# Attention stage of a four-layer graph network: rows of two tiles in every twelve picked on TensorE instead of two in sixteen, and the picked keys' product 128 columns wide

## The chip, the core and the metric

The kernel runs on one core of one Trainium2 chip. The metric is the device time of one execution in microseconds (us); lower is better.

## What is computed

Four layers of a graph network run on 3,125 nodes with 64 features and on 103,125 edges (two directions of 50,000 and one loop per node), sorted by their target node. Before each layer the nodes are normalised and cut at zero, and each layer's result is added to the nodes. The third layer is the attention that the change touches. Cut to what matters:

```python
q = (h @ Wq + bq).reshape(n, HEADS, C)
k = (h @ Wk + bk).reshape(n, HEADS, C)
v = (h @ Wv + bv).reshape(n, HEADS, C)
e = (edge_attr @ We).reshape(-1, HEADS, C)
qi, kj, vj = q[tgt], k[src] + e, v[src] + e
alpha = jnp.sum(qi * kj, axis=-1) / math.sqrt(C)
ex = jnp.exp(alpha - segment_max(alpha, tgt, n)[tgt])
a = ex / (segment_sum(ex, tgt, n)[tgt] + 1e-08)
agg = segment_sum(a[:, :, None] * vj, tgt, n)
```

For every edge the row of its source node (`src`) is needed; these are the rows that are gathered or picked.

## The kernel before, in words

The stages run one after the other: tables, dense matrices of the graph, layers 0 and 1, the attention's tables, the attention over the edges (`stage_attend`), the node part (`stage_nodes`), the messages of the last layer (`stage_messages`), and the output. The change lies in `stage_attend` and in the constants in front of it.

`stage_attend` cuts the edges into T1 = 403 tiles of 256 edges. A block is 64 target nodes, of which there are J2 = 49. A table made earlier lists V2 = 451 visits, each one tile with one block. Every engine walks the visits in a loop over `i`, with its own offsets: in iteration `i`, TensorE turns tile `t = i + 2`, scores visit `i`, makes picking products that belong to that iteration, and sums visit `i - 5`. I call one such iteration a step.

A tile gets the rows of its source nodes in one of two ways.

- Fetched tiles: GpSimd issues two indirect DMAs of 128 rows each from the row table in memory (L1594). A ring of eight semaphores lets it run at most eight fetched tiles ahead of what TensorE has turned (L1591), and another wait keeps it within the 64 tile slots (L1592). TensorE waits for the landing and for the edge attributes (L1617, L1618), and turns the tile with two transposes (L1620); ScalarE copies the result into `XF` (L1672).
- Picked tiles: the last two of every AG = 16 tiles, from tile 16 on (`picked`, L1321 to L1323), which makes 24 groups with 48 such tiles; the other 355 tiles are fetched. For a group the 512 source indices are loaded to all partitions as 256 KB by a DMA of SP (L1579), ScalarE turns them to float16 (L1687), VectorE compares them with the node numbers of each of the 25 chunks of 128 nodes (L1765, one 128x512 comparison each, eight buffers), and TensorE multiplies each result with that chunk of a table that holds every value as two float16 halves (L1645, 128x512, 25 of them into one bank). ScalarE copies the sum out (`hT`, L1694). In the step of the tile TensorE adds the two halves by a product with `comb`, two identities of 64x64 on top of each other: once with the 64 features on the partitions, for the keys (L1612), and twice with the edges on the partitions (L1614). ScalarE scales both into `XF` (L1669) and `rows` (L1670). The attributes of a picked tile come to `XF` by a DMA of SP (L1574).

`picks_of_step` (L1335 to L1338) spreads the 25 comparisons and products of a group over AG - 2 steps, starting PICK_AHEAD = 4 steps ahead of the group's first tile; the loads, the conversion L1687 and the copy L1694 have their steps by the same constants.

The rest of a step is the same for every tile. TensorE transposes the weights of the visit three steps behind (L1625), adds the mask of the block (two products, L1634), the scores (L1637), and sums with two products (L1655; before a picked tile's sum it waits for that tile's copy, L1652). VectorE makes the mask (L1712), the maximum (L1739), three small updates (L1745, L1750, L1759) and the sum (L1756). ScalarE copies the weights (L1675) and takes the exponentials (L1680, L1681). SP loads the queries (L1584) and the edge attributes (L1571).

Float32 products issue two matmuls each in the trace, so L1637 appears twice in a step and L1655 four times.

The constants of the schedule are these; nothing is planned by costs:

```python
AG = 16
AHOT = 8
TURN_AHEAD = 2
PICK_AHEAD = 4
```

`stage_messages` has a picking scheme of its own (GP = 6), which the change leaves alone; only its semaphore offsets Q0 and N0 follow the number of groups in `PICKS`.

Of the kernel before, what the change touches and what calls it, by code (L numbers as in the profile page):

```python
# [8 lines left out]
F16 = mybir.dt.float16  # L9
# [8 lines left out]
P = 128  # L18
NODES = 3125
EDGES = 103125  # L20
D = 64
# [7 lines left out]
TE = 256  # L29
# [43 lines left out]
RT = 64  # L73
# [1183 lines left out]
ONE = D + DE  # L1257
# [5 lines left out]
def landed(t, each=1):  # L1263

    return (t // R + 1) * (16 * each)
# [27 lines left out]
def wait(eng, sem, n):  # L1293

    if not isinstance(n, int) or n > 0:
        eng.wait_ge(sem, n)
# [10 lines left out]

CENTER = NODES // 2
SHIFTS = 5
AG = 16  # L1310
AHOT = 8
TURN_AHEAD = 2
MASK_AHEAD = 4
# [1 line left out]
SUM_BEHIND = 5  # L1315
# [5 lines left out]
def picked(t):  # L1321

    return t >= AG and t % AG >= AG - 2 and t - t % AG + AG <= T1  # L1323


FETCHED = [t for t in range(T1) if not picked(t)]
PICKS = [t for t in range(0, T1, AG) if picked(t + AG - 2)]


def fetched_before(t):  # L1330

    return sum(not picked(u) for u in range(t))


def picks_of_step(i):  # L1335

    return [(q, a) for q, t in enumerate(PICKS) for u in range(AG - 2) if i == t - PICK_AHEAD + u
            for a in range(u * NCH // (AG - 2), (u + 1) * NCH // (AG - 2))]  # L1338


def step_of_tile(t):

    return t + 1


def step_of_weights(v):

    return v + P_BEHIND + TURN_AHEAD + 1
# [162 lines left out]
def stage_attend(nc, m, keep, x_out, q_out, ea, ea_t, src, x_t, q_t):  # L1511
# [4 lines left out]
    with ExitStack() as ctx:  # L1516
        sem = lambda n: ctx.enter_context(nc.semaphore(n))
        take = Take(m.big)
# [6 lines left out]
        XF = take(RT * TE).rearrange("p (t e) -> p t e", t=RT)  # L1525
# [7 lines left out]
        psK = [m.PB[i][0:XW, 0:TE] for i in range(2)]  # L1533
# [3 lines left out]
        psR = [m.PB[5 + i][:, TE:TE + 2 * D].rearrange("p (s d) -> p s d", s=2) for i in range(2)]  # L1537
        psH = m.PB[7]
        hT = take(TE).bitcast(F16)
        key = take(TE).bitcast(F16)  # L1540
        comb = take(D // 2).bitcast(F16)
        down, wexp = take(1), take(1).bitcast(I32)
        keyI = more(2 * TE).bitcast(I32)
        hot = [more(TE).bitcast(F16) for _ in range(AHOT)]
# [18 lines left out]
        @block.sync  # L1563
        def _(sp):
            own = Walk(nc, m, "block", mybir.EngineType.SP)
            for v in range(V2):
                if v < T1:
                    wait(sp, turned, step_of_tile(v - R))
                    wait(sp, summed, v - RT + J2)
                    tile = ea[v:v + 1, :, :].rearrange("t p n -> p (t n)").rearrange("p (s c) -> p s c", s=2)  # L1570
                    sp.dma_start(rows[:, v % RT, :, D:D + DE], tile).then_inc(m.landed_e[v % R], 16)  # L1571
                    if picked(v):
                        sp.wait_ge(init, 2)
                        sp.dma_start(XF[D:D + DE, v % RT, :], ea_t[v, :, :]).then_inc(landed_x[v % 2], 16)  # L1574
                    if v + PICK_AHEAD in PICKS:
                        q = PICKS.index(v + PICK_AHEAD)
                        wait(sp, key_ready, q)
                        edges = src[(v + PICK_AHEAD + AG - 2) * TE:(v + PICK_AHEAD + AG) * TE]
                        sp.dma_start(keyI, edges.partition_broadcast(P)).then_inc(key_landed, 16)  # L1579
                j = own.of(v)  # L1580
                wait(sp, scored, v - R + 1)
                if v == 0:
                    sp.wait_ge(q_out, 16 * NG)
                sp.dma_start(qT[v % R], q_t[bass.ds(j, 1), :, :].rearrange("j p n -> p (j n)")).then_inc(m.landed_q[v % R], 16)  # L1584
# [12 lines left out]
        @block.tensor  # L1597
        def _(pe):
            pe.wait_ge(init, 1)
            own = Walk(nc, m, "slot", mybir.EngineType.PE)  # L1600
            for i in range(-TURN_AHEAD, V2 + SUM_BEHIND):
                t, u = i + TURN_AHEAD, i - P_BEHIND
                if u < V2:
                    wait(pe, copied, t - 1)
                if t < T1 and picked(t):
                    q = PICKS.index(t - t % AG)
                    e = (t % AG - (AG - 2)) * TE
                    pe.wait_ge(m.landed_e[t % R], landed(t))
                    pe.wait_ge(landed_x[t % 2], LATE_LOADS[t % 2] + 16 * (q + 1))
                    pe.wait_ge(h_copied, q + 1)  # L1610
                    wait(pe, acc_ready, i - SUM_BEHIND - 1)
                    pe.matmul(psK[t % 2][0:D, :], comb, hT[:, e:e + TE], start=True, stop=True)  # L1612
                    for s in range(2):
                        ins = pe.matmul(psR[(i - SUM_BEHIND) % 2][:, s, :], hT[:, e + s * P:e + (s + 1) * P], comb, start=True, stop=True)  # L1614
                elif t < T1:
                    n = fetched_before(t)
                    pe.wait_ge(m.landed_g[n % R], landed(n, 2))  # L1617
                    pe.wait_ge(m.landed_e[t % R], landed(t))  # L1618
                    for s in range(2):
                        ins = pe.transpose(psK[t % 2][:, s * P:(s + 1) * P], rows[:, t % RT, s, :], m.ident[:, :])  # L1620
                if 0 <= u < V2:
                    pe.wait_ge(exp_ready, u + 1)
                    for s in range(2):
                        part = slice(s * P, (s + 1) * P)
                        ins = pe.transpose(psT[t % 2][:, part], Pm[u % 6][:, part], m.ident[:, :])  # L1625
                if u < V2:
                    ins.then_inc(turned, 1)
                v = i
                if 0 <= v < V2:
                    slot = own.of(v)  # L1630
                    pe.wait_ge(oh_ready, v + 1)
                    wait(pe, exp_ready, v - 2)
                    for e in range(2):
                        pe.matmul(psS[v % 3][:, e * P:(e + 1) * P], oh[v % 8][:, e, :], pen, start=(e == 0), stop=False)  # L1634
                    pe.wait_ge(m.landed_q[v % R], landed(v))
                    pe.wait_ge(copied, step_of_tile(min(v, T1 - 1)))
                    pe.matmul(psS[v % 3], qT[v % R][0:XW, :], XF[0:XW, bass.ds(slot, 1), :].rearrange("p t e -> p (t e)"),  # L1637
                              start=False, stop=True).then_inc(scored, 1)
                for q, a in picks_of_step(i):
                    n = q * NCH + a  # L1640
                    if a == 0:
                        pe.wait_ge(init, 2)
                        wait(pe, h_copied, q)
                    pe.wait_ge(hot_ready, n + 1)
                    pe.matmul(psH, table[:, a, :, :].rearrange("p s d -> p (s d)"), hot[n % AHOT],  # L1645
                              start=(a == 0), stop=(a == NCH - 1)).then_inc(hot_used, 1)
                v = i - SUM_BEHIND
                if 0 <= v < V2:
                    slot = own.of(v)
                    pe.wait_ge(copied, step_of_weights(v))  # L1650
                    if t < T1 and picked(t):
                        pe.wait_ge(copied, step_of_tile(t))  # L1652
                    wait(pe, acc_ready, v - 1)
                    for s in range(2):
                        ins = pe.matmul(psA[v % 2], PT[v % 4][:, s * P:(s + 1) * P],  # L1655
                                        rows[:, bass.ds(slot, 1), s, :].rearrange("p t c -> p (t c)"), start=(s == 0), stop=(s == 1))
                    ins.then_inc(summed, 1)
# [39 lines left out]
        def _(dve):  # L1697
# [18 lines left out]
            def split():  # L1716

                dve.wait_ge(q_out, 16 * NG)
                for t in range(AG - 2, RT, AG):
                    dve.memset(XF[ONE:ONE + 1, t:t + 2, :], 1.0)  # L1720
                dve.tensor_copy(down, downI)
                dve.tensor_copy(comb[0:D, :], m.ident[0:D, 0:D])
                dve.tensor_copy(comb[D:P, :], m.ident[D:P, D:P])
                chain(dve.tensor_scalar(wexp, gall.bitcast(I32), 0x7F800000, None, ALU.bitwise_and))
                chain(dve.tensor_scalar(wexp, wexp, float(87 << 23), None, ALU.max))
                chain(dve.tensor_scalar(m.scale.bitcast(I32), wexp, -1.0, float(268 << 23), ALU.mult, ALU.add))
                chain(dve.tensor_scalar(m.unscale.bitcast(I32), wexp, -float(14 << 23), None, ALU.add))
                chain(dve.tensor_scalar(table[:, :, 0, :], hn, m.scale, None, ALU.mult))
                dve.scalar_tensor_tensor(table[:, :, 1, :], hn, m.scale, table[:, :, 0, :], ALU.mult, ALU.subtract).then_inc(init, 1)

            for i in range(-MASK_AHEAD, V2 + SUM_BEHIND):
                if i == 3:
                    split()
# [650 lines left out]
```

## Time and profile before

| | |
|---|---|
| device time, three runs | 3196.3, 3214.78 and 3215.32 us, median 3214.78 us |
| profiled execution, first to last instruction | 3198.0 us |
| mean granted clock of TensorE in it | 0.937 |
| attention: first to last gather issued | 1390.3 to 2280.5 us |
| attention: fetched / picked tiles | 355 / 48 |

The page gives the profiled execution's span alone as its time. PE is TensorE's matmuls, PEld its weight loads, DVE is VectorE, ACT ScalarE, POOL GpSimd, SP SyncE. A busy share counts instructions, not issuing of DMAs; the indirect DMAs of GpSimd are shown as instructions of that engine.

### The profile page before, as it was taken

What the parts mean: (1) busy time and instruction counts of PE and PEld (TensorE: products, weight loads), DVE (VectorE), ACT (ScalarE), POOL (GpSimd) and SP (SyncE); (2) the same over time, 40 slices, a digit from 0 to 9 for tenths busy, and PEclk for the clock granted to TensorE, in tenths of its full rate; (3) what the DMA queues carried; (4) which work ended last, traced back from release to release, by engine and by line L of the source; (5) the groups of instructions that cost most, each with busy time, mean ns of one, the idle gap of its engine ahead of it and who ended that gap; (6) DMA issues with size and microseconds to landing.
All of it is one profiled execution on the core that took longest, in us unless ns stands there. A gap on an engine that the chain in (4) does not pass through costs nothing. (4 is left out here: it accounts for less than half of the span.)

```text
span 3198.0 us, 70441 instructions
## 1 busy us (share of the span) xinstructions
PE 2723.7 (85%) x18621; PEld 1834.2 (57%) x18621; DVE 2250.6 (70%) x6702; ACT 1612.0 (50%) x4685; POOL 1512.6 (47%) x1604
## 2 busy tenths in 40 slices
PE   2777777799998499759888888998986999999998
PEld 1566665355554244337777777776874555555556
DVE  6999998566665312657777777777887777777772
ACT  1788887033332000035555555555664666666666
POOL 2121122044443000067777777777405777777770
PEclk6999999899999799869999999999997999999995
DMA  1122222056557755543333333333203555445540
GB/s 38 73 91 89 91 89 89 21 195 204 196 197 257 270 238 238 223 102 80 84 81 81 82 85 79 83 83 82 63 21 98 127 131 131 127 128 130 131 112 12
DMA packets 446966, 378.15 MB, mean 118 GB/s; under 512 B 174376, under 2 KB 385416, under 8 KB 446632
## 3 DMA queue, kind: packets, MB, share of 16 engines
q1 hardware_dynamic: 396184, 315.64, 32.3%
q0 software_dynamic: 40896, 43.60, 6.7%
q10 hardware_dynamic: 9552, 14.75, 1.3%
q8 instruction: 175, 2.87, 0.4%
q14 instruction: 159, 1.30, 0.1%
HBM read 286.75 MB, written 87.03 MB: 117 GB/s over the span
## 5 line engine op out<-in xcount | busy, mean ns | idle before, releaser
L1594 POOL DMA_INDIRECT big<-row_table,src x710 | 675.0, 951 | 217.1 <-issue 171.6
L2080 POOL DMA_INDIRECT big<-message_table,src x542 | 532.6, 983 | 228.2 <-issue 154.2
L2119 PE MATMUL banks<-big 128*128 128x512 f16 x1650 | 422.6, 380 | 8.9 <-DVE big L2194 8.9
L2212 DVE TENSOR_SCALAR big<-big 128x2048 f16<-128x2048 f16 (+2 forms) x396 | 422.4, 1067 | 1.3 <-DMA big<-shifted_keys 0.7
L507 PE MATMUL banks<-work 128*128 128x226 f16 x1197 | 312.3, 261 | 104.2 <-ACT banks L538 41.4
L899 PE MATMUL banks<-big,work 128*128 128x512 f16 (+1 forms) x1750 | 350.0, 359 | 17.0 <-DVE work L1041 17.0
L964 POOL TENSOR_TENSOR work<-work 128x400 f16<-128x400 f32 x196 | 180.2, 945 | 280.5 <-DVE work L1033 220.3
L1739 DVE TENSOR_REDUCE big<-banks 128x1 f32<-128x256 f32 x451 | 190.2, 422 | 173.1 <-PE banks L1637 159.7
L1637 PE MATMUL banks<-big 97*128 x902 | 303.4, 419 | 0.7
L508 PE MATMUL banks<-work 128*128 128x200 f16 x1197 | 300.5, 251 | 0.0
L509 PE MATMUL banks<-work 128*128 128x200 f16 x1197 | 298.6, 249 | 0.0
L450 POOL COPY work<-work 128x100 f16<-128x100 f16 x120 | 86.2, 723 | 380.9 <-DVE work L473 361.8
L1680 ACT ACTIVATE big<-big 128x1 f32<-128x1 f32 x451 | 91.6, 203 | 346.5 <-DVE big L1750 336.2
L899 PEld LDWEIGHTS banks<-big,work 128*128 128x128 f16 x1750 | 157.9, 101 | 188.2 <-DVE work L1041 17.3
L2156 ACT ACTIVATE big<-iotaH,rel 128x64 f32<-128x64 f16 x902 | 258.5, 334 | 5.5 <-DVE big L2171 3.9
L2128 PEld LDWEIGHTS banks<-big 128*64 128x64 f32 x1804 | 148.4, 145 | 184.9 <-issue 183.9
L1115 PE MATMUL banks<-big,work 128*128 128x512 f16 x900 | 202.7, 386 | 55.8 <-DVE work L1199 52.0
L1620 PE MATMUL banks<-ident,big 128*97 128x128 f32 x710 | 145.9, 288 | 100.0 <-issue 68.2
L928 ACT CAST work<-work 128x400 f16<-128x400 f32 x196 | 100.8, 525 | 238.8 <-DMA work<-weights_dense 238.0
L2128 PE MATMUL banks<-big 128*64 x1804 | 212.5, 244 | 7.8 <-issue 2.8
L2119 PEld LDWEIGHTS banks<-big 128*128 128x128 f16 x1650 | 153.4, 98 | 114.2 <-DVE big L2194 9.2
L533 ACT ACTIVATE work<-banks 128x800 f32<-128x800 f32 x196 | 163.5, 834 | 97.7 <-PE banks L509 89.9
(373 smaller groups left out, 6143.4 us busy)
## 6 DMA issues: line engine op xcount, KB each, us to landing
big<-weights_halves SPq DMA_DIRECT2D x10, 6400.0 KB, 24.0
big<-shifted_keys SPq DMA_DIRECT2D x66, 640.0 KB
weights_dense<-work SPq DMA_DIRECT2D x196, 200.0 KB, 1.9
work<-weights_dense SPq DMA_DIRECT2D x196, 200.0 KB, 2.7
weights_halves<-work SPq DMA_DIRECT2D x98, 400.0 KB, 2.9
big<-q_table SPq DMA_DIRECT2D x451, 64.0 KB
big<-in_ef SPq DMA_DIRECT2D x403, 64.0 KB
big<-in_ea SPq DMA_DIRECT2D x403, 32.0 KB
```

Of the source, the lines that this page charges most:

```text
L507: pe.matmul(to(CW, CW + CAW), rows[:, 0, t, :], cols[:, t, :], start=False, stop=True, skip_group_check=True)
L508: pe.matmul(to(0, CW), rows[:, 1, t, :], cols[:, t, 0:CW], start=False, stop=True, skip_group_check=True)
L509: pe.matmul(to(0, CW), rows[:, 2, t, :], cols[:, t, 0:CW], start=False, stop=True, skip_group_check=True).then_inc(vis_done, 1)
L899: ins = pe.matmul(m.PB[c % 4][:, 0:width(c)], z[k][:, a, :, :], m.counts(c)[:, a, :], start=(a == 0), stop=(a == NCH - 1))
L1115: pe.matmul(out, z[l % 2][:, a, :, :], weights[:, :, s, a * BP:(a + 1) * BP], start=(a == 0 and s == 0), stop=False)
L1594: po.indirect_dma_start(rows[:, t % RT, s, 0:D], None, x_t.rearrange("a p c -> (a p) c"), bass.IndirectOffsetOnAxis(ap=m.src2[:, s, t:t + ...
L1637: pe.matmul(psS[v % 3], qT[v % R][0:XW, :], XF[0:XW, bass.ds(slot, 1), :].rearrange("p t e -> p (t e)"), start=False, stop=True).then_inc( ...
L2080: po.indirect_dma_start(G[n % R][:, s, :], None, g_t.rearrange("a p c -> (a p) c"), bass.IndirectOffsetOnAxis(ap=m.src2[:, s, t:t + 1], ax ...
L2119: pe.matmul(psH[q % 2], table[:, a, :, :].rearrange("p s d -> p (s d)"), hot[:, 2 * TE * a:2 * TE * (a + 1)], start=(a == 0), stop=(a == N ...
L2128: ins = pe.matmul(psA[v % 3], oh[v % 4][:, s, :], M[:, bass.ds(slot, 1), s, :].rearrange("p t c -> p (t c)"), start=(s == 0), stop=(s == 1))
L2156: ins = nc.scalar.activation(away[v % 2][:, s, :], m.iotaH[:, 0:BD], ACT.Abs, bias=m.rel2[:, s, v:v + 1], scale=-1.0)
L2212: dve.tensor_scalar(hot[:, 2 * TE * a:2 * TE * (a + n)], key[q % 2][:, 0:n, :], place[:, BATCHES.index((a, n)):BATCHES.index((a, n)) + 1], ...
```

## The change

One constant goes from 16 to 12. The two picked tiles are then the last two of every twelve tiles, from tile 12 on: 32 groups with 64 picked tiles, and 339 fetched ones. A group's 25 comparisons and 25 products are spread over ten steps (two and three in turn) instead of fourteen. `comb` is twice as wide (the two identities also side by side), so that the keys' product writes all 128 partitions of its bank, of which ScalarE reads the first 64 as before; the product for the rows uses the first 64 columns. The memsets that put the constant row into `XF` follow the new places; four are left in number.

```diff
-AG = 16
+AG = 12
...
-        comb = take(D // 2).bitcast(F16)
+        comb = take(D).bitcast(F16)
...
-                    pe.matmul(psK[t % 2][0:D, :], comb, hT[:, e:e + TE], start=True, stop=True)
+                    pe.matmul(m.PB[t % 2][:, 0:TE], comb, hT[:, e:e + TE], start=True, stop=True)
                     for s in range(2):
-                        ins = pe.matmul(psR[(i - SUM_BEHIND) % 2][:, s, :], hT[:, e + s * P:e + (s + 1) * P], comb, start=True, stop=True)
+                        ins = pe.matmul(psR[(i - SUM_BEHIND) % 2][:, s, :], hT[:, e + s * P:e + (s + 1) * P], comb[:, 0:D], start=True, stop=True)
...
-                for t in range(AG - 2, RT, AG):
-                    dve.memset(XF[ONE:ONE + 1, t:t + 2, :], 1.0)
+                for t in range(RT):
+                    if picked(t) and t % 2 == 0:
+                        dve.memset(XF[ONE:ONE + 1, t:t + 2, :], 1.0)
                 dve.tensor_copy(down, downI)
-                dve.tensor_copy(comb[0:D, :], m.ident[0:D, 0:D])
-                dve.tensor_copy(comb[D:P, :], m.ident[D:P, D:P])
+                for half in range(2):
+                    dve.tensor_copy(comb[0:D, half * D:(half + 1) * D], m.ident[0:D, 0:D])
+                    dve.tensor_copy(comb[D:P, half * D:(half + 1) * D], m.ident[D:P, D:P])
```

## Rows read from the trace of the kernel before

**Rows 1.** The page's first line: span and instructions.

```profile
span 3198.0 us, 70441 instructions
```

**Rows 2.** Windows: busy us (instructions) of PE, PEld, DVE, ACT, POOL; PE clock, DMA share, GB/s.

```profile
1500.00:2200.00 700.00, 623.31 (x4368) 503.32 (x4367) 532.46 (x2733) 396.16 (x1356) 529.77 (x559) 0.98 0.39 82
2290.00:2350.00 60.00, 59.70 (x474) 55.42 (x473) 57.87 (x326) 38.88 (x143) 0.00 (x0) 1.00 0.17 47
```

**Rows 3.** The gathers' line L1594: durations, first and last start; idle (us, times).

```profile
L1594 POOL DMA_INDIRECT big<-row_table,src x710: 940/944/1870, 1390.3 to 2280.5; - x178
...
  issue: 171.6, 563
  PE banks L1655: 29.0, 95
```

**Rows 4.** Timeline of GpSimd: start, duration, instruction; in brackets the idle time ahead.

```profile
1395.52 0.94 POOL L1594 DMA_INDIRECT big<-row_table,src  x1 [0.30 <-issue]
1396.77 0.94 POOL L1594 DMA_INDIRECT big<-row_table,src  x1 [0.31 <-issue]
...
1949.27 0.94 POOL L1594 DMA_INDIRECT big<-row_table,src  x1 [0.30 <-issue]
1950.52 0.94 POOL L1594 DMA_INDIRECT big<-row_table,src  x1 [0.31 <-issue]
...
1954.26 0.94 POOL L1594 DMA_INDIRECT big<-row_table,src  x1 [0.30 <-issue]
```

**Rows 5.** Timeline of TensorE: steps of fetched tiles, with two products L1645 and with one.

```profile
1933.20 0.38 PE L1620 MATMUL banks<-ident,big 128*97 128x128 f32 x2
...
1934.24 0.60 PE L1645 MATMUL banks<-work 128*128 128x512 f16 x2
...
1935.09 0.38 PE L1620 MATMUL banks<-ident,big 128*97 128x128 f32 x2
...
1936.13 0.38 PE L1645 MATMUL banks<-work 128*128 128x512 f16 x1
...
1936.76 0.38 PE L1620 MATMUL banks<-ident,big 128*97 128x128 f32 x2
```

**Rows 6.** Timeline of TensorE: last two fetched tiles of a group and its picked ones.

```profile
1887.69 0.39 PE L1620 MATMUL banks<-ident,big 128*97 128x128 f32 x2
...
1891.37 0.27 PE L1612 MATMUL banks<-big 128*64 128x256 f16 x1 [0.58 <-ACT big L1694]
...
1893.27 0.68 PE L1655 MATMUL banks<-big,work 128*128 x4 [0.41 <-ACT big L1675]
...
1895.82 0.68 PE L1655 MATMUL banks<-big 128*128 x4 [0.19 <-ACT work L1675]
1896.34 0.39 PE L1620 MATMUL banks<-ident,big 128*97 128x128 f32 x2
```

**Rows 7.** Timeline of TensorE: the turns of tiles 250 and 252.

```profile
1951.91 0.43 PE L1620 MATMUL banks<-ident,big 128*97 128x128 f32 x2 [0.48 <-issue]
...
1958.53 0.43 PE L1620 MATMUL banks<-ident,big 128*97 128x128 f32 x2 [2.15 <-issue]
```

**Rows 8.** Lines L1612, L1645, L1765 and L1687: ns min/median/max, first and last start.

```profile
L1612 PEld LDWEIGHTS banks<-big x48: 106/106/128, 1469.6 to 2280.8; 128*64 128x64 f16 x48
L1612 PE MATMUL banks<-big x48: 269/297/423, 1469.6 to 2280.8; 128*64 128x256 f16 x48
...
L1645 PE MATMUL banks<-work x600: 377/381/634, 1431.3 to 2274.1; 128*128 128x512 f16 x150
...
L1765 DVE TENSOR_SCALAR work<-big x600: 273/284/523, 1427.8 to 2271.8; 128x512 f16<-128x512 f16 x150
...
L1687 ACT ACTIVATE big<-work,big x24: 707/710/711, 1426.3 to 2239.6; 128x512 f16<-128x512 int32 x24
```

**Rows 9.** Timeline of VectorE: from one maximum to the next, with two comparisons between.

```profile
1938.24 0.41 DVE L1739 TENSOR_REDUCE big<-banks 128x1 f32<-128x256 f32 x1
...
1939.89 0.42 DVE L1739 TENSOR_REDUCE big<-banks 128x1 f32<-128x256 f32 x1
```

## The prediction, written before the changed kernel ran

> **What bounds the kernel now.** I read the span first, then the busy shares by stretch, then the line of the gathers with its idle time, and last the timelines of GpSimd and TensorE. The change can act only in the attention, which takes about 890 of 3198.0 us [rows 1, 3]. In its even part, 700 us long, TensorE is busy 623.31 us (89%) and GpSimd 529.77 us (76%) [rows 2]. By the shares TensorE looks like the bound. The gathers' own line says otherwise: one takes 944 ns, and the idle time ahead of it is 171.6 us in 563 cases, which is 0.305 us each, and where a release by TensorE is named instead it is 29.0 us in 95 cases, again 0.305 us each [rows 3]. So the gap is the same whoever is named, and GpSimd never waits for anybody. It issues a gather each 1.25 us from start to end [rows 4]; 559 in 700 us make 1.252 us [rows 2]. That queue is full, and it sets the pace.
>
> TensorE confirms this from the other side. Running freely, its step takes 1.89 us with two picking products and 1.67 us with one [rows 5]. So a product costs 0.22 us and a step without one 1.45 us. Later in a group it stops ahead of a tile's transposes with the releaser named "issue" (0.48 us, 2.15 us) [rows 7]: those are waits for landings. By count, the second gather of tile 250 is the one issued at 1949.27, done at 1950.21, and its turn starts 1.70 us later; that is about the landing's normal delay [rows 4, 7].
>
> **The two budgets, before.** A group of 16 tiles has 28 gathers, 28 x 1.252 = 35.06 us. On TensorE it has twelve steps with 22 products, 12 x 1.45 + 22 x 0.22 = 22.2 us, and the end of the group: the last two fetched tiles and the two picked ones, from 1887.69 to 1896.34, 8.65 us, with three products and the waits for ScalarE in it (0.58, 0.41 and 0.19 us) [rows 6]. Together 30.9 us, 4.2 us less than GpSimd needs. That is the margin that the change spends.
>
> **The change, part by part.**
>
> Gathers. 355 fetched tiles become 339, so 16 x 2 = 32 gathers go: 32 x 1.252 = 40.1 us less on the engine that sets the pace. A group of 12 has 20 gathers, 25.04 us.
>
> TensorE. A group of 12 has eight steps with 20 products, 8 x 1.45 + 20 x 0.22 = 16.0 us, and the same end. In it five products stand instead of three; they go ahead of L1655, where the engine now waits 0.41 and 0.19 us, so of the 0.44 us most is hidden (bounds 0 and 0.44, I take 0.05). The relative places of the conversion L1687, the copy L1694 and the picked steps are the same for either AG, as all are counted from the group's end, so these waits stay. Sum 16.0 + 8.65 + 0.05 = 24.7 us. That is below 25.04, but the margin is 0.3 us and no longer 4.2.
>
> The wide product. Before, a 64-column product has its weight load start together with it, at 106 ns, and the matmul of 256 columns shows 297 ns, hardly less than the 381 ns of a 512-column one [rows 8]. No row shows a 128-wide one in this place. Bounds per tile: it costs no more than a whole extra product slot, +0.22 us [rows 5], and saves no more than its own 0.30 us [rows 8]. I take a saving of 0.1 us, the length of the exposed load; in both tiles 0.2 us a group, on TensorE, where it is margin and not time while GpSimd sets the pace.
>
> The Trainium skill, "TensorE: Matmul & The Clock Gate", section "Weight-path perf modes — Fast Weight Load (FWL) and DoubleRow", has weights load about twice as fast when there are 128 columns and they aren't float32. By it the load would shrink to an estimated 50 ns and the sum would be the same.
>
> VectorE. 8 x 25 = 200 more comparisons. With two of them its step runs 1.65 us from maximum to maximum without idling [rows 9]. A third adds at most 0.28 us [rows 8], 1.93 us, while TensorE's step with three products is 1.45 + 3 x 0.22 = 2.11 us. So TensorE hides it; if that cover went, ten steps with 25 comparisons would take no more than 16.5 + 5 x 0.28 = 17.9 us, which is still shorter than those steps on TensorE.
>
> ScalarE and SP. Eight more conversions of 0.71 us [rows 8] and eight more 256 KB key loads. ScalarE is busy 57% in the even part and the DMA engines 39% [rows 2]; behind the conversion on ScalarE stand the copies of the next tile, which is already in the 8.65 us. The key load used to be issued about the middle of a group, when TensorE had caught up with the landings; now it is issued two or three steps behind the picked tiles, when the landings are furthest ahead. On SP nothing waits anew. 0 us, at worst 32 late landings (below).
>
> Start. Two more small copies on VectorE ahead of the first picking, and each group's first picking two steps nearer to the start of its tiles. GpSimd waits for none of this, as its gathers run on at the same spacing from 1390.3 us [rows 3, 4]. 0 us, with 0 and 0.5 us as bounds.
>
> What is late next. A landing is sometimes late: tile 252's second gather ended at 1954.26 + 0.94 = 1955.20 and its turn began 3.33 us behind it, 1.6 us later than normal [rows 4, 7]. Where the landings lead TensorE by more than that, such a delay vanishes. After the change TensorE lags so long in each group that it nearly always has this cover, and GpSimd, which may run eight tiles ahead, isn't held. What one late landing costs is carried as lag and won back by 0.3 to 0.5 us a group. I put 2 us for the lag left at the end (0 to 8).
>
> Sum: -40.1 + 2 = -38 us. Against the profiled execution 3198.0 - 38 = 3160 us; it lies 16.8 us below the median of the runs, and I move the median by the same amount: 3214.78 - 38 = 3177 us, 1.2% less. The likeliest case by itself reaches from -44 to -32 us.
>
> **Rivals.**
>
> A. TensorE becomes the bound. If its group takes 25.5 us and more instead of 24.7 (stalls of 0.1 us in its free steps are enough), then 32 groups at 25.5 to 26.1 give back 32 x (25.5 - 25.04) = 15 to 34 us, and the gain is 6 to 25 us: 3190 to 3209 us. For it: the two budgets are within 2%, and 89% was busy before. Against it: the free steps repeat at 1.89 us.
>
> B. Slower. Late landings aren't covered and aren't won back. The old pace for twelve tiles is 35.06 x 12 / 16 = 26.3 us. If each group loses 1.6 us as at tile 252, it takes 25.04 + 1.6 = 26.6 us, and 32 x 0.3 = 10 us are added: about 3225 us. It decides from 1.3 us of loss in a group. For it: one such delay in a group is common in the second half of the old groups. Against it: there TensorE had no lag behind the landings to cover it.
>
> C. Comparisons on VectorE hold GpSimd. In the trace the spacing is 1.25 us before any comparison runs (1395.52) and 1.25 us between steps with two of them (1949.27) [rows 4], so nothing of the kind shows. If each of the 200 new ones took its 0.284 us from GpSimd, 57 us would come and 40 go: +17 us, 3232 us. The Trainium skill, "SBUF — State Buffer", section "Who interferes with whom", says that a VectorE instruction in a two-port mode, which a `tensor_scalar` like this comparison can enter, blocks GpSimd for its whole length; by that rule the change would lose, and the trace doesn't agree with it in these rows.
>
> D. The gain is larger, because the wide product and fewer stalls shorten the end as well: -44 us and beyond, 3170 us and less. It lies within the range.
>
> **Chances.** The forecast (with D) 0.67, A 0.25, B 0.05, C 0.03. About 1%, 32 us, is what a measurement of this kernel can tell from no change. The forecast lies mostly beyond it (0.62 of 0.67), A mostly within. So faster by over 1% 0.62, within 1% 0.32, slower 0.06. The range goes from 3214.78 - 60, with 16 of these for a median that falls at the lowest run shown, to 3207, which takes in most of A: 3155 to 3207 us.
>
> **What would show it.** The line L1594 with 678 gathers, 1.25 us apart and idle 0.305 us each time, the last one issued about 40 us earlier, at 2240. TensorE's waits named "issue" ahead of L1620, frequent before, almost gone, and its busy share in the even part up from 89% to some 97%. The end of a group still about 8.7 us. Wrong would be: idle times of GpSimd over 0.31 us (it is held by TensorE, rival A), steps of over 2.11 us with three products, or a spacing over 1.3 us (C).

## Result, and the profile after

The changed kernel takes 3180.84 us (median of five runs, 3175.61 to 3185.54) against 3207.67 us (3192.65 to 3215.32) for the kernel before: the recorded ratio is 0.9908, interval 0.9881 to 0.9935 (the two medians alone give 0.9916). It is faster, by 27 us where 38 us were forecast. That is 0.8 to 0.9%, just inside the bound of 1% beyond which I had put 0.62 of the chance. Of all executions that follow one counts as slow, the profiled one of narrow12, because it is over 1.5% longer than the fastest of its kernel; its granted clock, 0.941, is that of the others. The time itself fell within 4 us of the 3177 us forecast, and this flatters the forecast: the expected gain came almost whole, and a loss in a stage that I never looked at took part of it back.

The page after, first line, and the even part of the attention in the windows view (the columns of [rows 2]):

```profile
span 3174.7 us, 71147 instructions
```

```profile
1500.00:2200.00 700.00, 661.97 (x4752) 529.98 (x4751) 590.16 (x3025) 424.50 (x1443) 530.77 (x556) 1.00 0.40 88
```

TensorE is busy 95% of this stretch and no longer 89%; GpSimd issues 556 gathers in it, where it issued 559 [rows 2]. The gathers' own line answers to [rows 3]:

```profile
L1594 POOL DMA_INDIRECT big<-row_table,src x678: 940/944/1757, 1385.1 to 2239.7; - x170
...
  issue: 164.1, 538
  PE banks L1655: 22.9, 75
```

678 gathers, and the idle time ahead is still 0.305 us in either row: GpSimd still waits for nobody. From the first to the last it takes 854.6 us instead of 890.2 us, 35.6 us less. TensorE's steps with two and with three products, in its timeline, are 1.89 and 2.11 us, as worked out:

```profile
1954.31 0.38 PE L1620 MATMUL banks<-ident,big 128*97 128x128 f32 x2
1955.35 0.60 PE L1645 MATMUL banks<-work 128*128 128x512 f16 x2
1956.20 0.38 PE L1620 MATMUL banks<-ident,big 128*97 128x128 f32 x2
1957.24 0.81 PE L1645 MATMUL banks<-work 128*128 128x512 f16 x3
1958.31 0.38 PE L1620 MATMUL banks<-ident,big 128*97 128x128 f32 x2
```

Its waits for landings in 1500 to 2200 us, in the view of the waits (us in total, times, longest), shrank as forecast. The first line is of the kernel before, the second of the one after:

```profile
PE banks L1620 <- issue: 51.3, 52, 2.6
```

```profile
PE banks L1620 <- issue: 11.2, 9, 2.2
```

Cut by stage, the two profiled executions give this. The attention runs from the first gather to the last start of L1655, "the rest" from there to the end of the span.

| us | up to the first gather | attention | the rest | span |
|---|---|---|---|---|
| before | 1390.3 | 965.0 | 842.7 | 3198.0 |
| after | 1385.1 | 926.9 | 862.7 | 3174.7 |
| difference | -5.2 | -38.1 | +20.0 | -23.3 |

The attention gained the 38 us. The rest, where the code is the same but for the offsets of a semaphore, lost 20 us. The largest difference there is in the page's group of the message stage's gathers (busy us, mean ns, idle), before and after:

```profile
L2080 POOL DMA_INDIRECT big<-message_table,src x542 | 532.6, 983 | 228.2 <-issue 154.2
```

```profile
L2082 POOL DMA_INDIRECT big<-message_table,src x542 | 555.0, 1024 | 229.2 <-issue 156.1
```

The same 542 gathers are 22.4 us longer in sum. The timeline after shows one of the long ones. Here GpSimd, and below it VectorE's line L2214, the comparisons of that stage:

```profile
2953.68 2.05 POOL L2082 DMA_INDIRECT big<-message_table,src  x1 [0.32 <-issue]
2956.03 0.94 POOL L2082 DMA_INDIRECT big<-message_table,src  x1 [0.30 <-issue]
```

```profile
2954.07 0.73 DVE L2214 TENSOR_SCALAR big<-big 128x2048 f16<-128x2048 f16 x1
...
2954.87 0.73 DVE L2214 TENSOR_SCALAR big<-big 128x2048 f16<-128x2048 f16 x1
...
2955.66 1.53 DVE L2214 TENSOR_SCALAR big<-big 128x2560 f16<-128x2560 f16 x1
```

The gather begins ahead of two comparisons of 2048 elements that follow each other, and ends at 2955.73, 0.13 us behind the second. The next one lies under the comparison of 2560 elements and takes its normal 0.94 us. The smaller comparison is also the faster one by more than its size, 0.73 against 1.53 us, and even the batch of 3, 1536 elements, takes 0.995 us: 2048 elements run in another mode. This gave theory L: in that mode VectorE holds GpSimd, and how often depends on how the two fall on each other. Rivals were D, an outside disturbance of that one execution, and P, something fixed in the changed program.

The whole trace bears the example out. After the change 129 of the stage's 542 gathers last over 1.0 us, and 127 of them touch a comparison of 2048 elements. Every one of the 127 ends at one of two distances behind the end of such a comparison: 0.11 to 0.14 us (56) or 0.80 to 0.84 us (71). So a gather seems to need something that a fast comparison holds at two moments, by my estimate about 0.13 us behind its start and 0.13 us ahead of its end (0.944 - 0.82 and 0.944 - 0.13 us of its undisturbed length). A comparison that lies between the two costs nothing: of the 413 gathers that stay short, 92 touch a fast one.

### The profile page after: what moved, and what is told of

It reads as the page before. It is cut to its first block and busy times, and to the rows that moved or that the text cites. A ratio compares the mean times of both kernels' runs of the same rounds, so it can differ in the third digit from the quotient of the medians.

```text
span 3174.7 us, 71147 instructions
## 1 busy us (share of the span) xinstructions
PE 2736.6 (86%) x18837; PEld 1836.6 (58%) x18837; DVE 2285.4 (72%) x6904; ACT 1621.8 (51%) x4717; POOL 1526.0 (48%) x1572
## 5 line engine op out<-in xcount | busy, mean ns | idle before, releaser
L1594 POOL DMA_INDIRECT big<-row_table,src x678 | 649.1, 957 | 207.4 <-issue 164.1
L2082 POOL DMA_INDIRECT big<-message_table,src x542 | 555.0, 1024 | 229.2 <-issue 156.1
L2214 DVE TENSOR_SCALAR big<-big 128x2048 f16<-128x2048 f16 (+2 forms) x396 | 420.0, 1061 | 0.6 <-DMA big<-shifted_keys 0.3
L450 POOL COPY work<-work 128x100 f16<-128x100 f16 x120 | 103.2, 867 | 364.1 <-DVE work L473 345.0
L1645 PE MATMUL banks<-work 128*128 128x512 f16 x800 | 225.6, 379 | 0.0
L2208 DVE TENSOR_TENSOR big<-banks,big 128x128 f32<-128x128 f32 x271 | 77.7, 287 | 189.3 <-PE banks L2114 156.8
```

The costliest lines, as they stand in the source:

```text
L1594: po.indirect_dma_start(rows[:, t % RT, s, 0:D], None, x_t.rearrange("a p c -> (a p) c"), bass.IndirectOffsetOnAxis(ap=m.src2[:, s, t:t + ...
L2082: po.indirect_dma_start(G[n % R][:, s, :], None, g_t.rearrange("a p c -> (a p) c"), bass.IndirectOffsetOnAxis(ap=m.src2[:, s, t:t + 1], ax ...
L2214: dve.tensor_scalar(hot[:, 2 * TE * a:2 * TE * (a + n)], key[q % 2][:, 0:n, :], place[:, BATCHES.index((a, n)):BATCHES.index((a, n)) + 1], ...
```

## Experiments

All times are medians, and each ratio is against runs of the kernel before on the same chip. "Gathers busy" is the page's busy time of the 542 gathers of the message stage; 542 x 0.944 = 512 us is what they take undisturbed. In the expectations the attention and the rest were cut 2 to 4 us differently, at the end of TensorE's timeline that I had read by then.

**again12: the changed kernel once more.**

> The changed kernel once more. State of the question: in the profiled executions the attention got 38.2 us shorter, as forecast, but the stages behind it 20.1 us longer (845.8 to 865.9 us), where nothing was changed. Theory L (VectorE holds GpSimd in the messages stage): the loss depends on how VectorE's 2048-element comparisons fall on the gathers, so it varies from execution to execution; the attention again takes 922 to 926 us, the rest anything from 846 to 868 us. Rival D (an outside disturbance of that one profile): the rest is back at 846 us, the time at about 3157 us. Rival P (something fixed in the changed program, such as its instruction stream): the rest is 864 to 868 us every time.

3176.85 us, ratio 0.9902 (0.9865 to 0.9939), executions from 3169.01 to 3188.51. Attention 929.2, rest 863.1, gathers busy 554.6 us. Rival D falls: the loss came back to within a us. Rival P foretold just that and stands so far.

**narrow12: the product 64 columns wide.** The edit puts the three lines of `comb` and the two copies back.

```diff
-                    pe.matmul(m.PB[t % 2][:, 0:TE], comb, hT[:, e:e + TE], start=True, stop=True)
+                    pe.matmul(psK[t % 2][0:D, :], comb, hT[:, e:e + TE], start=True, stop=True)
```

> Two picked in twelve, but the keys' product 64 columns wide as before the change. The wide product saves 0.1 to 0.2 us in each of 64 picked tiles on TensorE. If GpSimd sets the pace, its gathers still take 854 to 856 us from first to last and the attention stays within 2 us of the changed kernel's 923.7 us. Rival T (TensorE has become the bound): the attention gets 6 to 13 us longer.

3170.84 us (3167.29 without the longest execution, as in the ratio), 0.9884 (0.9838 to 0.9931), but its executions run from 3156.03 to 3204.02. The profiled one was the longest: attention 931.1, rest 885.0, gathers busy 576.5 us. What this execution has above the others isn't put down to the edit. Against rival P speaks the spread within one program: 48 us, and still 40 us without the longest. For the attention neither expectation was met: it is 4.2 us longer than after the change and 1.9 us longer than in again12, over the 2 us of a GpSimd that sets the pace and under the 6 us of rival T. The gathers took 857.1 us, 1 us over their range. odd_narrow12 below comes back to this.

**odd12 and odd16: message comparisons in batches of 5, with two picked in twelve and in sixteen.**

```diff
-BATCHES = ((0, 5), (5, 4), (9, 5), (14, 3), (17, 4), (21, 4))
+BATCHES = ((0, 5), (5, 5), (10, 5), (15, 5), (20, 5), (25, 0))
...
                 for q, a, n in batch_of_step(i + 2):
+                    if not n:
+                        continue
```

> The changed kernel with the comparisons of the messages stage in five batches of 5 chunks instead of 5, 4, 5, 3, 4, 4. In the trace the batches of 4 (2048 elements) take 0.74 us and those of 5 (2560 elements) 1.53 us, so only the batches of 4 run in the fast mode in which VectorE may hold GpSimd. Theory L: without them no gather of that stage takes over 1.1 us, its 542 gathers take about 541 x 1.245 = 674 us from first to last instead of 697 (before) and 719 us (after), if VectorE's 1.4 us more of work in each group of six tiles doesn't become the bound; the total is 3125 to 3145 us. Rivals D and P: the gathers aren't faster, VectorE's extra work changes nothing or costs up to 20 us.

> The kernel before with the same five batches of 5 in the messages stage. Theory L: both the steady loss and the varying one go, so the time is 3165 to 3185 us, and the ratio of the five-batch kernels with twelve and with sixteen shows the change's own gain free of that stage: 38 us, 1.2%. Rivals D and P: the ratio is the one measured for the change, 0.991.

odd12: 3161.89 us, 0.9852 (0.9818 to 0.9885), executions only 8 us apart; attention 929.4, rest 845.0. odd16: 3195.71 us, 0.9964 (0.9943 to 0.9985); attention 964.3, rest 844.4. The group of the gathers and their idle time in odd12:

```profile
L2082 POOL DMA_INDIRECT big<-message_table,src x542 | 513.2, 947 | 240.6 <-issue 148.9
```

```profile
  issue: 148.9, 488
  POOLq L1773: 65.4, 1
  DVE big L2208: 26.3, 53
```

The long gathers are gone (513.2 us), but for two of 1.6 and 2.2 us at the start of the stage, where no fast comparison runs and where the kernels before and after have two as well. GpSimd now does wait for others: 26.3 us in 53 cases is 0.50 us each, over the gap of 0.305. In 2800 to 3050 us of odd12 TensorE is busy throughout, though VectorE has risen from 76% to 88%:

```profile
2800.00:3050.00 250.00, 250.00 (x1583) 139.15 (x1582) 220.80 (x365) 157.62 (x608) 183.31 (x195) 1.00 0.51 129
```

So the message stage is TensorE's as long as the gathers lose little, and that is why the absolute expectation missed: I expected 3125 to 3145 us from GpSimd's 674 us, it took 687.4 us at TensorE's pace. The kernels with batches of 5 differ by 33.8 us: that is the change's own worth, where I wrote 38.

**even12: five fast comparisons in a group instead of three.**

```diff
-BATCHES = ((0, 5), (5, 4), (9, 5), (14, 3), (17, 4), (21, 4))
+BATCHES = ((0, 4), (4, 4), (8, 4), (12, 4), (16, 5), (21, 4))
```

> The changed kernel with the messages' comparisons in batches of 4, 4, 4, 4, 5, 4: five fast 2048-element comparisons in a group instead of three, and 1.7 us less work on VectorE in each group of six tiles. Theory L: more of the gathers are held. The time above 944 ns, summed over the 542 gathers, was 20.1 us before, 42 us after (twice) and 0.4 us with batches of 5 alone; here it is over 50 us, and the time is above the changed kernel's 3177 us, at 3180 to 3210 us. Rival V (VectorE's own load is what delays the stage, not the mode): the sum falls below 42 us and the time below 3170 us.

3242.50 us, 1.0105 (1.0074 to 1.0135): slower than the kernel before, with less work on VectorE. Rest 926.7 us. Here 208 gathers last over 1.0 us; 206 of them touch a fast comparison, and all 206 end at one of the two distances.

```profile
L2082 POOL DMA_INDIRECT big<-message_table,src x542 | 617.8, 1140 | 230.4 <-issue 154.3
```

The direction was right, the size beyond the 3210 us that I had allowed. Rival V falls.

**one12: batches of 5, 5, 5, 3, 3, 4, a single fast comparison in a group.**

> The changed kernel with message batches of 5, 5, 5, 3, 3, 4: one fast comparison of 2048 elements in a group instead of three. Time above 944 ns summed over the stage's 542 gathers so far: 0.4 us with none of them, 20 to 64 us with three, 106 us with five. Theory L: it lies between, at 3 to 20 us, and since TensorE sets the stage's pace below about 20 us of such loss, the time is that of odd12, 3158 to 3166 us. If even one fast comparison set off the long holds, the sum is over 20 us and the time over 3170 us.

3165.94 us, 0.9859 (0.9819 to 0.9899). Gathers busy 531.7 us, a loss of 20 us at the upper end of what L allowed, and the rest is 844.6 us, as without any loss. The loss isn't in proportion to the fast comparisons: with one in a group it is as large as in the first profile of the kernel before with three.

**again16: the kernel before once more.**

> The kernel before once more. Its runs fall on two levels, about 3197 and 3214 us. Theory L: the levels are two patterns of the same holds in the messages stage. If the profiled execution is one of the upper level, its span is about 3214 us, the attention 964 to 965 us as before, the rest 858 to 862 us and the gathers' time above 944 ns about 35 to 42 us instead of 20.1. If it falls on the lower level, it repeats the first profile and this stays open.

The profiled execution was of the upper level: 3215.66 us, span 3213.8, attention 965.8, rest 861.7 us.

```profile
L2080 POOL DMA_INDIRECT big<-message_table,src x542 | 553.6, 1021 | 229.3 <-issue 154.3
```

So the kernel before has the same loss in a good half of its executions, and the profile I had read was of the others: of 82 executions in all, 32 lie at 3193 to 3204 us and 50 at 3205 to 3233, crowded about 3197 and 3215. The traces show what divides the levels. Apart from the two at the stage's start, the first profile has no gather over 1.5 us; again16 has 16, again12 18 and the one after the change 20, and each of these lies over two or more fast comparisons in a row. They lose 19 to 21 us above 944 ns each time, just the difference of the levels. one12, where no fast comparison follows another, has none. Together:

| message gathers busy, us | rest, us | from |
|---|---|---|
| 512.9 to 514.5 | 843.4 to 845.0 | the seven kernels with batches of 5 |
| 531.7 / 532.6 | 844.6 / 842.7 | one12 / before, first profile |
| 553.6 / 554.6 / 555.0 | 861.7 / 863.1 / 862.7 | again16 / again12 / after |
| 576.5 | 885.0 | narrow12 |
| 617.8 | 926.7 | even12 |

Up to about 20 us of loss cost nothing; beyond, each us of it is a us of the kernel (from 532.6 to 617.8 is 85 us, the rest grows by 84).

The next runs are about the attention alone, with batches of 5 so that the message stage is quiet.

**odd_ag14 and odd_ag10: two picked in fourteen and in ten** (`AG = 14`, `AG = 10`).

> Batches of 5 in the messages stage as in odd12, two picked in fourteen. 28 groups, 347 fetched tiles, 694 gathers: 16 gathers more than with twelve, 16 x 1.262 = 20 us. If GpSimd still sets the attention's pace at twelve, this lies midway between odd12 (3162) and odd16 (3196): 3178 us. Rival T (TensorE is the bound at twelve): nearer to odd12, under 3172 us.

> Batches of 5 as in odd12, two picked in ten. 39 groups, 325 fetched tiles, 650 gathers. GpSimd would need 16 x 1.262 = 20.2 us for a group of ten; TensorE needs eight steps' worth of plain work (six fetched with 20 products, 6 x 1.45 + 20 x 0.22 = 13.1) and the end of a group 8.7: 21.8 us. So TensorE is the bound: 2.18 us a tile against 2.10 with twelve, about 30 us slower than odd12, 3185 to 3195 us, and GpSimd shows idle times well over 0.31 us. If GpSimd were still the bound, it would be 28 x 1.262 = 35 us faster than odd12.

odd_ag14: 3181.93 us, 0.9915 (0.9885 to 0.9944), attention 950.4 us. My count was off: there are 27 groups and 698 gathers. GpSimd took 877.9 us for them, 23.4 us more than with twelve, and the time is 20 us above odd12, about as GpSimd's pace has it. odd_ag10: 3190.69 us, 0.9939 (0.9915 to 0.9963), attention 958.1 us. GpSimd now is held, 0.75 us in each of 116 cases:

```profile
L1594 POOL DMA_INDIRECT big<-row_table,src x650: 940/944/1752, 1385.4 to 2261.7; - x163
...
  issue: 151.8, 484
  PE banks L1625: 86.9, 116
```

TensorE is the bound at ten, GpSimd at fourteen and, with 0.305 us everywhere, at twelve, where the two meet.

**odd_wide16 and odd_narrow12: the wide product by itself, with sixteen and taken away with twelve.**

> Batches of 5 as in odd16, two picked in sixteen, only the keys' product 128 columns wide. With GpSimd as the bound and 4 us of room on TensorE in each group, the wide product changes nothing: 3196 us, within 3 us of odd16. If it did help by itself, by 0.1 to 0.2 us in each of 48 tiles, 3186 to 3191 us.

> Batches of 5 in the messages stage as in odd12, and the keys' product 64 columns wide as before the change. The messages stage is then the same in both, so this shows the wide product's worth by itself, with twelve. If GpSimd sets the attention's pace: within 3 us of odd12 (3162). If TensorE does: 6 to 13 us slower, 3168 to 3175 us.

odd_wide16: 3197.98 us (odd16 3195.71), attention 964.4 against 964.3: nothing, as expected. odd_narrow12: 3164.50 us, 0.9861 (0.9831 to 0.9890), attention 933.1 against 929.4. The total can't tell it from odd12. Of the attention's 3.7 us GpSimd's own pace has 2.7: its gathers take 857.2 us from first to last and not 854.5, and their median is 947 ns and not 944, as in again16 and even12 too, so the width isn't its reason. narrow12 (946 ns) is of the same kind. What is left for the wide product with twelve is about 1 us, and no run tells it from nothing. On TensorE the saving itself is plain. In its timeline after, the next product follows the wide one at 0.11 us, where a narrow one took 0.23 us before the change (1925.92 to 1926.15, in the same kind of step); these are also the medians over all 64 and all 48 picked tiles:

```profile
1876.52 0.27 PE L1612 MATMUL banks<-big 128*128 128x256 f16 x1
1876.63 0.22 PE L1614 MATMUL banks<-big 128*128 128x64 f16 x2
```

```profile
1925.92 0.30 PE L1612 MATMUL banks<-big 128*64 128x256 f16 x1
1926.15 0.23 PE L1614 MATMUL banks<-big 128*128 128x64 f16 x2
```

**double12: odd12 with each comparison of the attention made twice.**

```diff
+                    chain(dve.tensor_scalar(hot[n % AHOT], key, float(P * a - CENTER), None, ALU.is_equal))
                     dve.tensor_scalar(hot[n % AHOT], key, float(P * a - CENTER), None, ALU.is_equal).then_inc(hot_ready, 1)
```

> odd12 with every comparison of the attention (128x512) made twice into the same buffer, the second behind the first: 800 more of the comparisons of which the change adds 200. The gathers' time above 944 ns, summed over the attention, was 3.4 to 6.6 us with 600 comparisons and 7.3 to 9.0 us with 800 (wide product). Rival C in small (each comparison holds GpSimd a little, about 20 ns): with 1600 it is 20 to 30 us, whatever paces the stage. If the comparisons don't hold the gathers: it stays under 12 us. The time itself grows either way, because VectorE gets 800 x about 0.25 us more to do and its steps with two and three picks then take 2.2 to 2.7 us: 3185 to 3290 us.

3332.79 us, 1.0371 (1.0324 to 1.0419), more than I had allowed: VectorE is busy 95% of 1500 to 2200 us and sets the pace, since each doubled comparison also waits for the first (`chain`). The question was another:

```profile
L1594 POOL DMA_INDIRECT big<-row_table,src x678 | 646.2, 953 | 373.5 <-PE banks L1625 193.8 <-issue 147.3 <-PE banks L1655 31.5
```

The gathers are busy 646.2 us, against 649.1 us in odd12: twice the comparisons lost less. By the expectation the short comparisons wouldn't hold the gathers at all. But it took a hold for something that comes with every comparison, and the message stage shows that the phase decides. The kept traces settle it. In the one after the change:

```profile
1942.04 0.47 DVE L1767 TENSOR_SCALAR work<-big 128x512 f16<-128x512 f16 x2
```

```profile
1942.31 1.03 POOL L1594 DMA_INDIRECT big<-row_table,src  x1 [0.30 <-issue]
1943.64 0.94 POOL L1594 DMA_INDIRECT big<-row_table,src  x1 [0.30 <-issue]
```

The first gather begins under the second of two comparisons and ends 0.83 us behind it, the longer distance of the message stage. Counted over the attention, 111 gathers begin under a comparison that runs on for 0.15 us or more, and 105 of these last over 0.97 us; only 4 others do. The 105 end 0.81 to 0.83 us behind their comparison, and the 111 account for 7.9 of the 9.6 us by which the stage's gathers exceed their median. In the kernel before it is 43 of 46 gathers and 3.2 of 5.3 us; in double12, where VectorE sets the pace and the two engines fall on each other differently, 28 of 67 and 2.5 of 4.9 us. So the short comparisons do hold gathers, by 0.03 to 0.14 us each.

## Why the prediction was right, and where it was wrong

What bounds the attention: right. GpSimd set the pace before and does after, at nearly the same spacing (890.2 us for 709 steps, 1.256 us each, and 854.6 us for 677, 1.262).

The gathers, -40.1 us: 35.6 us in the profile. 32 x 1.25 us are gone, but the rest of them have become longer: their mean is 957 ns and no longer 951. 678 x 6 ns = 4.1 us, about the difference. In all kernels with sixteen the mean is 951 or 952 ns, with fourteen 954, with twelve 957 to 961, but for double12's 953. The reason is the comparisons: they lengthen 105 gathers after the change and 43 before it, and the loss that falls to them grows from 3.2 to 7.9 us. This term of the sum was too large by 4 us, because it left the length of a gather as it was.

TensorE's group, 24.7 against 25.04 us, with a margin of 0.3: right, as the held GpSimd at ten and the free one at twelve show. The end of a group, put at 8.65 us from one picture of it, takes 8.9 us at the median of all 32 (9.1 before), which makes TensorE's group an estimated 24.9 us. That it would hardly stop for landings was right (11.2 us from 51.3). The lag left at the end, put at +2 us, was a gain instead: the last turn starts at 2242.42, 1.8 us behind its gather, before the change 4.7 us (2286.15 behind 2281.43). So -35.6 and -2.9 us make -38.5 us; the profile shows -38.1. That the forecast of -38 fits so well is partly luck: the gathers gave 4 us too little and the lag 5 us too much. In the runs with batches of 5 the attention's gain is 34.9 us and the whole 33.8 us.

The wide product: the saving of 0.1 us a tile is 0.12 in the timeline. The size was right and its reason wasn't: the weight load didn't vanish or shrink to an estimated 50 ns, it shows 126 ns at the median where the narrow one showed 106; what came earlier is the start of the next product. That the saving would be only margin holds with sixteen (nothing), and with twelve as far as the runs can tell (about 1 us).

Rival C: I had its mechanism, and gave it 0.03. The step that failed is "nothing of the kind shows". It is true of the five gathers in [rows 4] and of no more: in the same stage of the same trace 43 gathers were held by comparisons of 512 elements. And I didn't look at the same pair of engines in the message stage, whose mean gather was 983 ns against 951 in the page of the kernel before. The price was wrong too: 57 us assumed a hold for the whole length of every new comparison, and it came to about 5 us, as only a comparison that covers one of the two moments holds a gather, and only for what is left of it. The Trainium skill, "SBUF — State Buffer", section "Who interferes with whom", says that whichever of GpSimd and a VectorE instruction in a two-port mode issues first has the shared ports for its whole length, and the other is blocked. The gather that ends 0.13 us behind the second comparison agrees with the block, and so do the runs without such comparisons; but that gather began 0.39 us ahead of the first of them and was held all the same, so who issues first doesn't decide here. In the Trainium skill's "VectorE: DVE Perf Modes", section "What auto-detection actually checks", the two-port modes need outermost dimensions that are both even or equal; a batch of 4 or 5 is that dimension on the source's side, and this agrees with 2048 elements in 0.73 us and 2560 in 1.53 us. The comparisons of 512 elements belong to the fast ones by their time: on the line through 1536 elements (0.995 us) and 2560 (1.53 us) 512 would take an estimated 0.46 us, and they take 0.284.

The sum for the median was the other wrong step: "I move the median by the same amount". The runs of the kernel before, 3196.3, 3214.78 and 3215.32 us, were two levels and not a spread, and the profiled execution was of the lower one. The changed kernel was on the upper level in both profiles. Level against level, 3214 to 3177, it gains 37 us (39 us by the profiled spans, again16's 3213.8 to 3174.7); the profiles compare lower with upper and show 23; the medians mix them. Rivals A and B fell: GpSimd was never held at twelve, and late landings were nearly all covered.

What the levels are made of is shown, gathers caught by two fast comparisons in a row. What stays open is why the changed kernel falls on the upper level in both of its profiles and, by their times, in nearly all of its eleven executions, and the kernel before in a good half of its own. The code of the message stage is the same, and narrow12 spreads over 48 us. That the phase depends on how the engines enter the stage is only argued.

The best version is odd12, which beats both: the change together with batches of 5, 3161.89 us, 1.5% below the kernel before and 15 us below the changed kernel on the same chip.

## What to carry to other kernels

Find the pace-setter by idle time that is the same whoever is named as releaser, then give each engine a budget per group; the optimum lies where the two budgets meet, and one step beyond it the time rises again. Before a median is moved by a forecast, see whether the runs form levels, and explain the level first: it may be worth as much as the change. Where GpSimd gathers and VectorE works in a fast mode, compare the mean gather of each stage with the shortest, and the end of each long gather with the end of the fast instruction beside it; long fast instructions back to back cost more than the slower form of the same work. A test that adds more of an instruction also shifts the engines against each other, so it can't by itself clear that instruction.

## What was unexpected about the hardware

- Two fast comparisons of 0.73 us in a row made a gather of 0.94 us last 2.05 us; five such comparisons in a group of six tiles cost 84 us of the rest against three in the lower level's pattern (926.7 against 842.7 us).
- Held gathers end at one of two distances behind the fast comparison, 0.11 to 0.14 or 0.80 to 0.84 us. Comparisons of 512 elements (0.284 us) do it too, with the longer distance; it costs so little (7.9 us in 678 gathers) because little of a comparison is left when a gather needs what it holds.
- Less work on VectorE made the kernel slower (even12, 3242.50 us) and more work faster (odd12, 3161.89 us).
- Behind a product of 256 columns with 64 columns of weights the next product starts 0.23 us later, with 128 columns of weights 0.11 us later (medians of 48 and 64).
